# Moving the turn, the rank products, the scatters and the first block table of layer 0's routing to later places in a written-out order

## The chip, the cores and the metric

The kernel runs on one core of a Trainium2 chip. The metric is the device time of one execution in microseconds (us); lower is better. A core has five engines, each of which works through its own list of instructions in order: TensorE (PE, matrix products and transposes), VectorE (DVE), ScalarE (ACT), GpSimd (POOL) and SyncE (SP, which here only issues DMAs). The engines wait for each other through semaphores.

## The reference

Two layers, each of them a cross-attention and a mixture of experts, over 32 sequences of 128 tokens with 128 features; each sequence attends to a context of 77 rows. In float32:

```python
x = x + tanh(g_xattn[0]) * attn0(layernorm(x), ctx)    # 8 heads of 64
x = x + tanh(g_ffn[0])   * moe0(layernorm(x))          # 8 experts, top 2, silu(a) * b, biases
x = x + tanh(g_xattn[1]) * attn1(layernorm(x), ctx)    # 16 heads of 8
x = x + tanh(g_ffn[1])   * moe1(layernorm(x))          # 8 experts, top 2, gelu
```

In `moe0` the scores of a token are `x @ Wr.T + br`; the two experts with the largest `scores + biases_N` are taken, and their softmax weights are scaled to a sum of one.

## The kernel before, in words

All engines follow one list, `order()`. Each element is a task such as `("rank", 0, g)`; every engine loops over the whole list and issues its own part of each task, or nothing. The place of a task in the list is therefore its place in the queue of every engine that has a part in it. Semaphore waits inside the tasks keep the data right.

Layer 0's attention is made by `attention0_steps`, one step u for each sequence, and four more at the end that overlap with the experts. A step holds these tasks in this order:

- `score0(u)`: six matmuls (L977) into two PSUM banks, then VectorE's minimum of each row, `row_max` (L1475), and a subtraction (L1478)
- `k0`: products of the keys for the next group of four sequences (PE L914 to L916, a copy on ACT L1264, the remainder on VectorE L1444), in up to three places of a step, named by `more[0]` to `more[2]`
- `exp0(u)`: four exponentials on ACT (L1304) and one over the first half (L1308)
- `weigh0(u - 2)`: ten matmuls (L1019) and VectorE's addition to `x_res` (L1497)
- `v0`: one product of values (PE), copied out by ACT as `vo` (L1314) and stored by SP. A second one, in every fourth step, comes after `turn0`
- `divide0(u)`: VectorE's `row_sum` (L1488) and reciprocal (L1491), POOL's division of `prob` (L1846)
- `turn0(u - 1)`: ten transposes of the divided `prob` (L1001), copied out by ACT as `prob_t` (L1329)
- `bias0(u)`, the third `k0`, `norm` or `normalize` of the next group
- the routing tasks due in this step, `tasks.get(u, [])`

The routing tasks belong to layer 0's experts and run under the attention. For a group g of four sequences, whose attention is done by step 4g + 5, `route_tasks` puts them at steps u = 4g + 6 plus an offset from `steps0`:

- `mnorm` (0): VectorE's statistics, POOL's `m_rstd` (L1887, L1889)
- `mnormalize` (1): VectorE's `m_shift` (L1533), then ACT's four copies to `xm` (L1297)
- `mturn` (2): four transposes on PE (L1113), copied by ACT to `xm_t` (L1355)
- `route` (3): eight matmuls (L1121), then VectorE's `scores`, `ranked` and the eight largest
- `pick` (4): VectorE finds the two experts of each token and counts (L1564 to L1586), POOL L1896 and L1899
- `rank` (5): five matmuls (L1134 to L1137) that give each token its place with its expert, then four operations on VectorE (L1593 to L1601), the last of which writes `row`
- `lead` (6): the weights of the two experts
- `scatter` j = 0 to 3 (5, 6, 7, 8): two indirect DMAs each on POOL (L1918), which write the normalized rows to `x_rows` at the places in `row`; they wait for `row` and `xm`

After group 4 (FIRST_GROUPS) the first table of blocks is made: `totals` (5), one matmul and VectorE; `blocks` in three pieces (6, 6, 6), VectorE alone (L1679 to L1711); `block_bias` (7), PE matmuls (L1151) and a copy on VectorE (L1715). SP's `fetch` tasks, which begin at the end of step 31, need the table's `row_of` and the landed scatters of groups 0 to 4.

PSUM has eight banks, and `bank_of` names that of each task. `mturn`, `route` and `rank` of groups 0 to 4 and the first `totals` use V_BANK, the one of `v0`; for the later groups, and for `block_bias`, it is ROUTE_BANK. A task on PE waits until the previous user of its bank in the list has been read: for `rank` in its old place this is the `vo` copy of the same step. ACT's `vo` copy comes after `exp0` in ACT's queue, and `exp0` waits for `row_max`.

Of the kernel before, what the change touches and what calls it, by code (L numbers as in the profile page):

```python
# [35 lines left out]
GS = 4  # L36
# [84 lines left out]
def route_tasks(layer, spacing, lag, steps, tables):  # L121

    at = {}
    for g in range(NG):
        u = spacing * g + lag
        for kind, step in zip(("mnorm", "mnormalize", "mturn", "route", "pick", "rank", "lead"), steps[g][0]):
            if g >= ROUTED[layer] and kind == "rank":
                continue  # L130
            at.setdefault(u + step, []).append((kind, layer, g))
            if g >= ROUTED[layer] and kind == "lead":
                at.setdefault(u + step, []).append(("expert_w",))
        if g + 1 in PART_GROUPS[layer]:
            part = PART_GROUPS[layer].index(g + 1)
            total, table, bias = tables[part]
            at.setdefault(u + total, []).append(("totals", layer, part))
            for e in range(NEXP if part == PARTS - 1 else 0):
                at.setdefault(u + total + e // (2 + 2 * layer), []).append(("tail", layer, e))
            for piece, step in enumerate(table):  # L140
                at.setdefault(u + step, []).append(("blocks", layer, part, piece))
            if layer == 0:
                at.setdefault(u + bias, []).append(("block_bias", layer, part))
        for j, step in enumerate(steps[g][1] if g < ROUTED[layer] else ()):
            at.setdefault(u + step, []).append(("scatter", layer, g, j))

    last = ("blocks", "lead") if layer == 0 else ("scatter", "blocks", "expert_w")
    return {u: sorted(step, key=lambda t: t[0] in last) for u, step in at.items()}


def value_halves():

    begun, out = 2, []
    for u in range(NSEQ):
        last = ((min(u + 2, NSEQ) * NKEY) - 1) // P
        n = min(max(2 * (last + 1), (5 * (u + 1) + 13) // 4), 2 * CTX_BLOCKS)
        out.append([("v0", k // 2, k % 2) for k in range(begun, n)])
        begun = n  # L160
    return out


def attention0_steps(tasks):
    values = value_halves()
    background = [("ctx", i) for i in range(2, CTX_SETS)] + [("weights1",), ("tables", 0)]
    background += [("expert", 0, e) for e in range(NEXP)] + [("tables", 1)]
    for u in range(NSEQ + 4):
        step = []
        more = prepare_attention0_at(u) if u < NSEQ else ([], [], [], [])  # L170
        if u < NSEQ:
            step += [("score0", u)] + more[0] + [("exp0", u)]
        if 0 <= u - 2 < NSEQ:
            step.append(("weigh0", u - 2))
        if u < NSEQ:
            step += [("v0_load", u)] + values[u][:1] + [("divide0", u)] + more[1]
        if 0 <= u - 1 < NSEQ:
            step.append(("turn0", u - 1))
        if u < NSEQ:
            step += values[u][1:] + [("bias0", u)] + more[2]  # L180
        step += more[3] + tasks.get(u, [])
        if background:
            step.append(background.pop(0))
        if u == NSEQ - 1:
            step += [("fetch", i) for i in range(AHEAD)]
        yield step
# [41 lines left out]
def prepare_attention0(g):  # L228
    out = [("norm", g)]
    for head in range(NH0):  # L230
        out.append(("k0", g, head))
        if head == 2:
            out.append(("normalize", g))
        if head == 5:
            out.append(("xt", g))
    return out


def prepare_attention0_at(u):

    g = (u + 1) // GS + 1 if u >= GS - 1 else 1
    if g >= NG:
        return [], [], [], []
    keys = ((3, 2, 1, 2) if g > 1 else (3, 3, 2, 0))
    turn = u % GS
    before = sum(keys[i] for i in ((3, 0, 1, 2) if g > 1 else (0, 1, 2))[:(turn + 1) % GS if g > 1 else turn])
    places = [[("k0", g, before + n)] for n in range(keys[turn])]
    if turn == 2:
        places.append([("xt", g)])
    places += [[]] * (3 - len(places))  # L250
    return places + [[("norm", g)] if turn == 0 else [("normalize", g)] if turn == 1 else []]
# [29 lines left out]
def first_keys_and_queries():  # L281

    loads = [[[("k_load", g, piece)] for piece in range(6)] for g in (0, 1)]
    clears = [[("clear", 1, heads)] for heads in range(HEAD_SETS)] + [[], []]
    out = [[("v1_ones",)]] + [[("clear", 0, heads)] for heads in range(HEAD_SETS)] + [[("k1", 0)], []]
    for load, clear in zip(loads[0], clears):
        out += [load, clear]
    out += [[("k1", 1)], []]
    for load in loads[1]:
        out += [load, []]  # L290
    return out + [[("norm", NG)], [], [("normalize", NG)], [("xt", NG)], [("q1", 0)], [("q_load", 0)]]


def dense_tasks(experts):

    return [t for e in experts for t in (("dense_up", e, 0), ("dense_up", e, 1), ("dense_down", e))]
# [60 lines left out]
def order():  # L357

    first = prepare_attention0(0)
    out = [first[0], ("turn_weight", 0), ("turn_weight", 1), ("ctx", 0), ("wqk", 0), ("wqk", 1), ("turn_weight", 2)]  # L360
    out += first[1:] + [("wvo", 0), ("wvo", 1), ("ctx", 1), ("v0", 0, 0), ("v0", 0, 1), ("gates",)]
    steps0 = [((0, 1, 2, 3, 4, 5, 6), (5, 6, 7, 8))] * 5 + [((0, 1, 2, 3, 4, 5, 6), (5, 6, 7, 8)), ((0, 1, 2, 3, 3, 4, 5), (5, 5, 5, 5)), ((0, 1, 2, 3, 4, 5, 6), (5, 6, 7, 8))]
    steps1 = [((0, 1, 3, 5, 6, 7, 9), (9, 11, 13, 15))] * 5 + [((0, 1, 3, 5, 6, 7, 9), (8, 9, 10, 11)), ((0, 1, 2, 3, 4, 5, 6), (6, 6, 7, 7)), ((0, 1, 3, 5, 6, 7, 9), (9, 11, 13, 15))]
    tasks = [route_tasks(0, GS, 6, steps0, ((5, (6, 6, 6), 7), (5, (6, 6, 6), 7))),
             route_tasks(1, 2 * GS, 13, steps1, ((7, (8, 8, 8), 0), (5, (6, 6, 6), 0)))]
    after0 = [[("expert", 1, e)] for e in range(NEXP)] + first_keys_and_queries()
    phases = [(attention0_steps(tasks[0]), NSEQ), (expert_steps(0, tasks[0], NSEQ + 4, after0), BLOCKS[0] + 2),
              (attention1_steps(tasks[1]), U1 + 1), (expert_steps(1, tasks[1], U1 + 5, []), BLOCKS[1])]
    begun = 0
    for i, (phase, alone) in enumerate(phases):  # L370
        after = phases[i + 1][0] if i + 1 < len(phases) else iter(())
        for _ in range(alone - begun):
            out += next(phase)
        begun = 0
        for step in phase:
            out += step
            out += next(after, [])
            begun += 1
        if i + 1 < len(phases):
            out += next(after)  # L380
            begun += 1
    late = dense_tasks(range(DENSE_LATE, NEXP))
    out += late[:-1] + [("load_last", q) for q in range(LAST // 2)]
    out += late[-1:] + [("dense_out", j) for j in range(GS)] + [("combine_last", n) for n in range(LAST)]
    apart = {t[1:] for t in out if t[0] == "rest"}
    return [u for t in out for u in ([t, ("rest",) + t] if t[0] in SPLIT_KINDS and t not in apart else [t])]


def flamingo_two_layers(nc, a, out):
    plan = order()  # L390

    splits = [t for t in plan if t[0] in SPLIT_KINDS]
# [1562 lines left out]
```

## Time and profile before

| what | value |
|---|---|
| median of 3 runs | 788.54 us (787.5 to 790.2) |
| the profiled execution's own time | 795.85 us |
| its span, first to last instruction | 794.1 us |
| mean granted TensorE clock | 0.933 of full speed |
| PE busy | 647.0 us, 81% of the span |
| VectorE busy | 556.0 us, 70% |
| ScalarE busy | 442.0 us, 56% |
| GpSimd busy | 448.4 us, 56% |

The profiled execution is 7.3 us longer than the median, so differences are taken within it. Layer 0's attention fills the span up to about 240 us; the edit touches steps from 86 us on. Times in the rows below are microseconds from the start of the span.

### The profile page before, as it was taken

Reading aid. Unit: us, or ns where it says so; the run is one execution under the profiler, and the core shown is the slowest. Engines: PE = TensorE matmul, PEld = TensorE weight load, DVE = VectorE, ACT = ScalarE, POOL = GpSimd, SP = SyncE. Lnnn points to the kernel's source line nnn. Section 1 sums busy time; section 2 is a strip of 40 time slices with the busy share of each in tenths; the row PEclk is TensorE's granted clock in tenths of the full one; section 3 lists DMA queues with packets and bytes.
Section 4 is the critical chain, followed back from the end, with each engine's and each line's share of the span. In section 5 each row is a group of like instructions: output and inputs, shape, how many; then the busy total and the mean of one; then the engine's idle time right before and its main releaser. Section 6 shows DMA issues by size and latency. Waiting matters only on the chain.

```text
span 794.1 us, 16522 instructions
## 1 busy us (share of the span) xinstructions
PE 647.0 (81%) x4501; PEld 584.0 (74%) x4501; DVE 556.0 (70%) x1971; ACT 442.0 (56%) x1275; POOL 448.4 (56%) x665
## 2 busy tenths in 40 slices
PE   6888888899766767978688899889879875898886
PEld 5677778888666657877677788878768874787775
DVE  3367688887874566876787889888878755444564
ACT  2476767677434434655556776767665542433452
POOL 4035357776667565875445334767656665565541
PEclk9999999998978788999997999999999996999999
DMA  9446667454422223434352435535413013332444
GB/s 261 117 115 171 174 172 182 124 154 110 127 72 87 62 79 113 110 93 119 106 156 76 114 78 107 122 85 103 113 58 84 31 34 93 102 89 79 135 145 153
DMA packets 127383, 89.48 MB, mean 113 GB/s; under 512 B 30996, under 2 KB 116276, under 8 KB 127260
## 3 DMA queue, kind: packets, MB, share of 16 engines
q1 hardware_dynamic: 110844, 64.93, 32.1%
q0 software_dynamic: 8128, 17.65, 6.8%
q10 hardware_dynamic: 8320, 5.85, 2.6%
q8 instruction: 38, 0.62, 0.3%
q14 instruction: 53, 0.43, 0.2%
HBM read 50.73 MB, written 39.85 MB: 114 GB/s over the span
## 4 chain that ended last, share of the span: by engine, by line
PE 39%; DVE 21%; issue 12%; ACT 11%; SPq 5%; another core or an unknown queue 4%; DMA 3%; POOL 2%; DVEq 1%; ACTq 0%; POOLq 0%
PE banks L1171 7%; PE banks L1191 5%; PE banks L1034 5%; SPq L824 3%; DMA v_rows<-vo 3%; DVE row_max L1428 3%; PE banks L914 2%; PE banks L1001 2%; PE banks L977 2%; PE banks L1212 2%; PE banks L1019 2%; DVE hidden L1743 2%; DVE up L1735 2%; DVE x_res L1767 2%
## 5 line engine op out<-in xcount | busy, mean ns | idle before, releaser
L1925 POOL DMA_INDIRECT y_rows<-y_sb,result_at x134 | 131.1, 978 | 107.9 <-DVE result_at L1723 46.5
L1171 PE MATMUL banks<-xb,up 128*128 128x128 f32 x820 | 127.8, 297 | 47.1 <-DVE hidden L1743 22.4
L1171 PEld LDWEIGHTS banks<-xb,up 128*128 128x128 f32 x820 | 112.8, 207 | 61.5 <-issue 33.7
L1918 POOL DMA_INDIRECT x_rows<-xm,row x120 | 120.5, 1004 | 31.6 <-issue 28.5
L1880 POOL TENSOR_TENSOR v_flat<-v_raw,row_head 104x64 f32<-104x64 f32 (+1 forms) x128 | 55.6, 461 | 73.1 <-ACT v_raw L1345 72.1
L1191 PE MATMUL banks<-down,hidden 128*128 x536 | 87.6, 289 | 8.9 <-DVE y_sb L1760 4.6
L1329 ACT ACTIVATE prob_t<-banks 128x512 f32<-128x512 f32 x192 | 73.3, 439 | 28.7 <-PE banks L1001 24.8
L1034 PE MATMUL banks<-v_flat,prob_t 128*128 128x108 f32 (+2 forms) x640 | 86.5, 284 | 3.3 <-ACT prob_t L1329 1.3
L1034 PEld LDWEIGHTS banks<-v_flat,prob_t 128*128 128x128 f32 (+1 forms) x640 | 79.7, 197 | 10.6 <-ACT prob_t L1329 6.8
L1383 ACT ACTIVATE gate<-banks,block_bias 128x128 f32<-128x128 f32 x142 | 44.4, 365 | 76.2 <-PE banks L1171 44.7
L1191 PEld LDWEIGHTS banks<-down,hidden 128*128 128x128 f32 x536 | 75.0, 202 | 12.0 <-issue 12.0
L1846 POOL TENSOR_TENSOR prob<-prob,inv_sum 128x616 f32<-128x616 f32 x32 | 39.1, 1223 | 57.8 <-DVE inv_sum L1491 57.6
L1743 DVE SCALAR_TENSOR_TENSOR hidden<-banks,block_bias,gate 128x128 f32<-128x128 f32 x142 | 42.8, 343 | 33.8 <-ACT gate L1383 27.5
L1428 DVE TENSOR_REDUCE row_max<-banks 128x8 f32<-128x616 f32 x64 | 50.4, 788 | 9.3 <-PE banks L993 9.3
L1001 PE MATMUL banks<-ident,prob 128*128 128x128 f32 (+1 forms) x375 | 56.3, 283 | 0.0
L1019 PE MATMUL banks<-vo_flat,prob_t 128*128 128x128 f32 (+1 forms) x320 | 47.4, 302 | 8.6 <-ACT prob_t L1329 6.6
L1735 DVE COPY up<-up 128x256 f32 x134 | 49.5, 370 | 6.9 <-issue 2.4
L1019 PEld LDWEIGHTS banks<-vo_flat,prob_t 128*128 128x128 f32 (+1 forms) x320 | 45.2, 217 | 9.7 <-ACT prob_t L1329 7.4
L1387 ACT ACTIVATE hidden<-banks 128x256 f32<-128x256 f32 x63 | 24.0, 382 | 45.9 <-PE banks L1171 35.8
L1760 DVE COPY y_sb<-banks 128x128 f32<-128x128 f32 x63 | 18.1, 287 | 44.5 <-PE banks L1191 32.3
L1304 ACT ACTIVATE prob<-banks,row_max 128x77 f32<-128x77 f32 x128 | 30.8, 324 | 32.7 <-issue 20.4
L1001 PEld LDWEIGHTS banks<-ident,prob 128*128 128x128 f32 (+1 forms) x375 | 46.2, 147 | 0.8 <-issue 0.2
(238 smaller groups left out, 1657.9 us busy)
## 6 DMA issues: line engine op xcount, KB each, us to landing
vo_flat<-v_rows SPq DMA_DIRECT2D x32, 256.0 KB
x_norm<-x_rows SPq DMA_DIRECT2D x74, 72.0 KB
v_rows<-vo SPq DMA_DIRECT2D x38, 128.0 KB
x_far<-x_rows SPq DMA_DIRECT2D x60, 72.0 KB
gathered<-y_rows ACTq DMA_DIRECT2D x32, 128.0 KB
q_rows<-up_raw SPq DMA_DIRECT2D x8, 512.0 KB, 2.8
q_even<-q_rows SPq DMA_DIRECT2D x12, 256.0 KB
q_odd<-q_rows SPq DMA_DIRECT2D x12, 256.0 KB
```

Source lines behind the costliest of these rows:

```text
L1001: done = pe.transpose(banks[0:chunk_rows[c], PT_BANK[k], c % 4 * SEQ:(c % 4 + 1) * SEQ], flat[:, c * P:c * P + chunk_rows[c]], ident[:, :])
L1019: done = pe.matmul(banks[:, O_BANK, 0:D], prob_t[0:rows, b % 2, c, :], vo_flat[0:rows, b % 2, c, :], start=c == 0, stop=c == CHUNKS - 1)
L1034: done = pe.matmul(banks[:, O_BANK, half * width:half * width + cols], prob_t[0:rows, u % 2, c, :], v1_flat[0:rows, first:first + cols], s ...
L1171: done = pe.matmul(banks[:, UP_BANK[i % 2], part * P:(part + 1) * P], block_w[:, i % WR, part // 2, part % 2 * P:(part % 2 + 1) * P], xb[: ...
L1191: done = pe.matmul(banks[:, Y_BANK[i % 2], 0:D], hidden[:, i % HR, half, :], of_expert(flat[:, (2 * layer + half) * D:], i, D), start=half ...
L1329: act.activation(dst, banks[0:rows, PT_BANK[k], 0:len(chunks) * SEQ], ACT.Copy).then_inc(sem("prob_t"))
L1428: dve.tensor_reduce(m_view, s_view, AX.X, ALU.max).then_inc(sem("row_max"))
L1735: dve.tensor_copy(block_w[:, i % WR, 1 - layer, :], src[:, bass.ds(at, HID1)]).then_inc(sem("block_w_dve"))
L1743: dve.scalar_tensor_tensor(hidden[:, i % HR, half, :], banks[:, UP_BANK[i % 2], (2 + half) * P:(3 + half) * P], block_bias[:, k, 2 + half, ...
L1880: pool.tensor_tensor(v1_rows[0:rows, b % 2, half, chunks[0]:chunks[-1] + 1, :, 0:DK1], v1_raw[0:rows, chunks[0]:chunks[-1] + 1, half, :, : ...
L1918: pool.indirect_dma_start(out=x_rows[layer][:, :], out_offset=bass.IndirectOffsetOnAxis(ap=row[:, n, c:c + 1], axis=0), in_=xm[:, i % 2, j ...
L1925: pool.indirect_dma_start(out=y_rows[layer][:, :], out_offset=bass.IndirectOffsetOnAxis(ap=result_at[:, i % (2 * YR):i % (2 * YR) + 1], ax ...
```

## The change

```diff
@@ attention0_steps
         if 0 <= u - 1 < NSEQ:
             step.append(("turn0", u - 1))
+        step += tasks.get(u - 0.5, [])
         if u < NSEQ:
             step += values[u][1:] + [("bias0", u)] + more[2]
         step += more[3] + tasks.get(u, [])
@@ order
-    steps0 = [((0, 1, 2, 3, 4, 5, 6), (5, 6, 7, 8))] * 5 + [...]
+    steps0 = [((0, 1, 2.5, 3, 4, 5.5, 6), (6, 7, 7, 8))] * 5 + [...]
-    tasks = [route_tasks(0, GS, 6, steps0, ((5, (6, 6, 6), 7), (5, (6, 6, 6), 7))),
+    tasks = [route_tasks(0, GS, 6, steps0, ((6, (7, 8, 8), 9), (5, (6, 6, 6), 7))),
```

An offset with a half is served in the middle of the next step, right after `turn0`. For groups 0 to 4 `mturn` is now there in step 4g + 9 (`route` is still at the end of that step) and `rank` in step 4g + 12. The scatters j = 0 and 1 are one step later, j = 2 and 3 where they were. Of the first table, `totals` moves from step 27 to 28, the three pieces of `blocks` from 28 to 29, 30 and 30, `block_bias` from 29 to 31. Groups 5 to 7, the second table and layer 1 are untouched, and no instruction is added or dropped.

## Rows read from the trace of the kernel before

**Rows 1.** The page, part 4: the chain that ended last, by engine.

```profile
PE 39%; DVE 21%; issue 12%; ACT 11%; SPq 5%; another core or an unknown queue 4%; DMA 3%; POOL 2%; DVEq 1%; ACTq 0%; POOLq 0%
```

**Rows 2.** Waits, 60 to 290 us: total us, times, longest.

```profile
ACT prob L1304 <- issue: 20.4, 6, 4.1
...
PE banks L1134 <- ACT vo L1314: 13.3, 5, 3.2
```

**Rows 3.** Timeline, steps 19 and 20: start, length, what [idle before it <- releaser].

```profile
153.40 0.77 DVE L1475 TENSOR_REDUCE row_max<-banks 128x8 f32<-128x616 f32 x1
...
154.20 0.97 ACT L1304 ACTIVATE prob<-banks,row_max 128x77 f32<-128x77 f32 x4 [2.77 <-issue]
...
155.39 0.61 ACT L1314 ACTIVATE vo<-banks 128x512 f32<-128x512 f32 x1
...
156.14 0.25 PE L1134 MATMUL banks<-picked,earlier 128*128 128x32 f32 x1 [2.41 <-ACT vo L1314]
...
157.06 0.19 DVE L1593 TENSOR_TENSOR rank_row<-banks,region 128x32 f32<-128x32 f32 x1
...
158.34 0.16 DVE L1533 SCALAR_TENSOR_TENSOR m_shift<-m_mean_var,m_rstd 128x4 f32<-128x4 f32 x1
158.53 1.65 ACT L1297 ACTIVATE xm<-x_res,m_shift,m_rstd 128x128 f32<-128x128 f32 x4 [1.56 <-DVE m_shift L1533]
...
161.72 0.79 DVE L1488 TENSOR_REDUCE row_sum<-prob 128x8 f32<-128x616 f32 x1 [0.44 <-ACT prob L1308]
...
163.62 0.48 DVE L1444 TENSOR_TENSOR k_t<-banks,k_t 128x308 fp32r<-128x308 f32 x1 [0.52 <-ACT k_t L1264]
```

**Rows 4.** Windows, `row_max` of step 4k+3 to 4k+5: length, busy by engine, PEclk, DMA.

```profile
153.40:165.14 11.74, 9.33 (x61) 8.97 (x59) 9.47 (x31) 8.31 (x25) 7.62 (x11) 0.85 0.52 136
177.46:190.79 13.33, 10.93 (x61) 10.42 (x59) 9.44 (x31) 8.44 (x25) 7.63 (x11) 0.74 0.46 120
sum 49.43, PE 39.37 PEld 37.77 DVE 37.88 ACT 33.69 POOL 29.60; mean PE 9.84 PEld 9.44 DVE 9.47 ACT 8.42 POOL 7.40
```

**Rows 5.** Timeline, the turn and the route of group 3.

```profile
163.47 0.60 ACT L1355 ACTIVATE xm_t<-banks 128x512 f32<-128x512 f32 x1
...
167.16 0.61 ACT L1314 ACTIVATE vo<-banks 128x512 f32<-128x512 f32 x1
...
167.82 1.06 PE L1121 MATMUL banks<-router,xm_t 128*128 128x8 f32 x8 [0.33 <-ACT vo L1314]
...
167.94 0.80 ACT L1329 ACTIVATE prob_t<-banks 128x512 f32<-128x512 f32 x2
```

**Rows 6.** Windows, `row_max` to `row_max` over a route, groups 0 and 3.

```profile
91.95:97.22 5.27, 4.58 (x35) 4.22 (x34) 4.90 (x16) 3.51 (x11) 2.89 (x4) 1.00 0.67 180
165.14:169.87 4.73, 4.41 (x34) 4.02 (x33) 4.08 (x17) 4.37 (x14) 3.93 (x7) 1.00 0.55 152
```

**Rows 7.** Source line L1121, whole span: idle before it, us and times.

```profile
  ACT xm_t L1355: 2.0, 2
```

**Rows 8.** Windows of VectorE alone, step 27 to 31: length, busy, PEclk, DMA.

```profile
203.11:237.15 34.04, 25.76 (x94) 0.82 0.30 85
```

**Rows 9.** Timeline, the block bias and the route of group 5.

```profile
221.40 1.88 PE L1121 MATMUL banks<-router,xm_t 128*128 128x8 f32 x8 [2.77 <-DVE block_bias L1715]
...
223.32 0.19 DVE L1546 TENSOR_TENSOR scores<-banks,router_b 128x32 f32<-128x32 f32 x1 [1.97 <-PE banks L1121]
...
225.06 0.80 DVE L1475 TENSOR_REDUCE row_max<-banks 128x8 f32<-128x616 f32 x1 [0.92 <-PE banks L977]
...
227.19 0.35 DVE L1497 SCALAR_TENSOR_TENSOR x_res<-banks,gates,x_res 128x128 f32<-128x128 f32 x1 [0.82 <-PE banks L1019]
```

**Rows 10.** Source line L1918, 100 to 235 us: ns min/median/max.

```profile
L1918 POOL DMA_INDIRECT x_rows<-xm,row x40: 957/995/1236, 109.7 to 231.7; - x40
```

**Rows 11.** Timeline of POOL, steps 21 and 22.

```profile
172.89 0.96 POOL L1918 DMA_INDIRECT x_rows<-xm,row  x1 [0.30 <-issue]
...
178.97 1.05 POOL L1889 TENSOR_TENSOR m_rstd<-m_rstd,minus_half 128x4 f32<-128x4 f32 x1
```

More of the change, by code:

```diff
@@ L361, in order @@
     out += first[1:] + [("wvo", 0), ("wvo", 1), ("ctx", 1), ("v0", 0, 0), ("v0", 0, 1), ("gates",)]
-    steps0 = [((0, 1, 2, 3, 4, 5, 6), (5, 6, 7, 8))] * 5 + [((0, 1, 2, 3, 4, 5, 6), (5, 6, 7, 8)), ((0, 1, 2, 3, 3, 4, 5), (5, 5, 5, 5)), ((0, 1, 2, 3, 4, 5, 6), (5, 6, 7, 8))]
+    steps0 = [((0, 1, 2.5, 3, 4, 5.5, 6), (6, 7, 7, 8))] * 5 + [((0, 1, 2, 3, 4, 5, 6), (5, 6, 7, 8)), ((0, 1, 2, 3, 3, 4, 5), (5, 5, 5, 5)), ((0, 1, 2, 3, 4, 5, 6), (5, 6, 7, 8))]
     steps1 = [((0, 1, 3, 5, 6, 7, 9), (9, 11, 13, 15))] * 5 + [((0, 1, 3, 5, 6, 7, 9), (8, 9, 10, 11)), ((0, 1, 2, 3, 4, 5, 6), (6, 6, 7, 7)), ((0, 1, 3, 5, 6, 7, 9), (9, 11, 13, 15))]
-    tasks = [route_tasks(0, GS, 6, steps0, ((5, (6, 6, 6), 7), (5, (6, 6, 6), 7))),
+    tasks = [route_tasks(0, GS, 6, steps0, ((6, (7, 8, 8), 9), (5, (6, 6, 6), 7))),
              route_tasks(1, 2 * GS, 13, steps1, ((7, (8, 8, 8), 0), (5, (6, 6, 6), 0)))]
```

## The prediction

> **What bounds the kernel now.** I read the page first, then the waits, then the stretch that the edit touches, engine by engine. The chain that ended last [rows 1] is spread over TensorE (PE), VectorE (DVE), "issue" and ScalarE (ACT): no engine is the bound by itself, so a saved microsecond counts only where a wait ends on it. The list of waits of layer 0's attention [rows 2] names the candidate: the rank products (L1134) stood 13.3 us, five times, for the copy of `vo` (L1314), which frees the one PSUM bank they share. Just above stand 20.4 us in which ACT had not begun `exp0` (L1304). The second explains the first, and the reader is to see it in [rows 3], step 19, the rank step of group 2. VectorE comes to the step's minimum (`row_max`, L1475) only at 153.40, because it still works on the picks and statistics of the step before. So ACT begins `exp0` at 154.20, copies `vo` at 155.39, and PE, idle for 2.41 us, starts the ranks at 156.14. VectorE then makes rows of them from 157.06 until `m_shift` at 158.34, ACT waits 1.56 us for `m_shift`, normalizes `xm`, and only then gets to the exponentials of step 20: `row_sum` at 161.72. The wait on PE is thus a result of VectorE's lateness, and the chain goes through VectorE and ACT. What I price is therefore the interval from one `row_max` to a later one. Step s is the s-th of the attention's steps, k0 the products of keys.
>
> **What the edit moves.** Nothing is added to or taken from the work. For groups 0 to 4 the turn of `xm` (four transposes on PE, one copy `xm_t` on ACT) goes from the end of step 4g+8 to the middle of 4g+9, where the route stays at the end; the ranks (five matmuls, four VectorE operations) go from the end of step 4g+11 to the middle of 4g+12; of the four scatter tasks (two indirect DMAs each, on POOL) the first two go one step later, so that step 4g+13 has two. The first table (totals, three pieces, block bias) goes from steps 27, 28, 29 to 28, 29, 30, 31.
>
> **The ranks, four times (groups 0 to 3).** Without the rank rows `m_shift` can come right after the k0 remainder at about 156.95, 1.4 us earlier (158.34 less 156.95; the four rank operations with their waits took 157.06 to 158.34 = 1.28 us). ACT's `xm`, `exp0` and `vo` and VectorE's `row_sum` all come 1.4 us earlier [rows 3]. Then the 1.28 us of rank rows come back, before the last k0 remainder of step 20, which stood idle for 0.52 us before it began at 163.62 [rows 3]. It takes up that gap: 1.4 - 1.28 + 0.52 = 0.64 us gained, of a stall of 2.41. PE now waits for the `vo` of step 20 instead: done with the turn at about 159.8, bank free at about 160.8, so about 1 us idle in place of 2.41. The four stretches from step 4k+3 to 4k+5 last 11.74 us for the one just worked through, 13.33 for the last, 49.43 in all [rows 4]: 49.43 - 4 x 11.74 = 2.47 us more than four of the middle one. In the last, PE's granted clock is 0.74 of full speed against 0.85, that is, it spent more time at the 1.2 GHz level after its idle stretch. With a stall of 1 us I expect it to stay at 2.4 GHz, and the excess to go. Together 4 x 0.64 + 2.47 = 5.0 us gained. Bounds: below, 1.0 (VectorE full, only part of the excess comes back); above, 13.3 (the whole wait [rows 2]).
>
> **The turn, five times.** This is the price. Today `xm_t` is copied at 163.47 in 0.60 us, where ACT has time, and the route at 167.82 waits only for `vo` (0.33 us) [rows 5]. Now the turn itself waits for the `vo` copy that ends at 167.77, and ACT has a k0 copy and two `prob_t` copies, until 168.74, before it comes to `xm_t`. The route directly behind on PE waits for that: 168.74 + 0.60 = 169.34 in place of 167.82, 1.5 us. After the route come three VectorE operations and then `row_max` of the next step, with nothing to hide behind; the stretch today takes 4.73 us [rows 6]. That such a wait exists is seen elsewhere in this trace: two routes waited for `xm_t`, 2.0 us together [rows 7]. In the first group the stretch is already 5.27 us [rows 6] since VectorE has a slow operation there; 0.5 us of the 1.5 is hidden by it. Sum: 4 x 1.5 + 1.0 = 7.0 us lost. Bounds: 0 (if the step found other cover) and 8.
>
> **The table and the last rank step.** From `row_max` of step 27 (203.11) to the rows of group 5 (237.15) VectorE is busy for 25.76 of 34.04 us [rows 8]. Its work is only dealt out differently, so what counts is the idle time. The block bias in front of the route of group 5 shares a bank with it: PE stood idle 2.77 us and came back at the low level of its clock (the eight matmuls took 1.88 us), VectorE stood idle 1.97, 0.92 and 0.82 us, 3.7 in all [rows 9]. With the block bias two steps later the route runs at once: 3.7 us gained. The new place of the block bias is in front of group 5's ranks, in step 31, same bank: its copy on VectorE, then five matmuls at the low clock, and VectorE waits about 1.1 us. Net 2.6 us gained; bounds 0.5 and 4.5. Groups 5 to 7 stay where they are, fetches wait for rows of the table at step 30 instead of 28, and begin in step 31 as before: nothing, unless the table ends late, which the gain here excludes.
>
> **The scatters.** POOL has the division of every step as well, and PE turns that result. Two more indirect DMAs now stand in front of the division of step 22. One takes 0.995 us [rows 10] and the queue 0.30 us to the next [rows 11], so POOL comes 2.6 us later to that division and to `m_rstd`, the last of what `m_shift` waits for. It ended at 180.02 (178.97 + 1.05 [rows 11]); with POOL's start 0.6 us earlier, 182.0. VectorE would ask for it 3.55 us after its `row_max`, at 177.46 + 0.86 + 3.55 = 181.9 (0.86 being 1.5 lost less 0.64 gained). So the cover is used up: 0.1 us late, four times, 0.4 us. The division itself has about a microsecond left.
>
> The Trainium skill bears on this. The 40 scatters of this attention took 957 to 1236 ns, whatever VectorE did beside them [rows 10]. "SBUF — State Buffer", section "SBUF: two separate sides", says that an indirect DMA issued from POOL can't write its descriptors while VectorE runs a copy that takes both ports, and gives 620 ns alone against about 3100 beside such a copy. By that rule the two added scatters could cost up to 5 us each time; the trace disagrees, and the sum goes by the rows.
>
> **Sum.** 7.0 + 0.4 - 5.0 - 2.6 = -0.2 us. It is made against the profiled execution, which took 795.85 us with a span of 794.1, 7.3 us above the median of the runs, 788.54; all terms are differences of short stretches, so I carry -0.2 over as it is: 788.3 us.
>
> **Rivals.** (a) *The turn is hidden*: ACT reaches `xm_t` sooner, or PE has other work. Then 7.0 falls away: 781.3 us. For it: PE waits only 0.33 us at the route now. Against: nothing stands between turn and route in the new order. 0.14. (b) *The rank wait comes back in full*: 13.3 in place of 5.0: 780.0 us. For it: it is the longest wait of PE. Against: [rows 3], VectorE and ACT are the late ones. 0.10. (c) *POOL becomes the bound*, the case on the other side. `m_rstd` passes 3.55 us after `row_max`; from there each microsecond costs four. If the six scatters ahead of it take 1.236 instead of 0.995 us, it is 1.4 us later, 5.8 us in all: 794.1 us. For it: the cover is gone. Against: the median lies near the low end of its rows. The skill's rule above would make this case larger. 0.12. (d) *The rank rows eat all that they free*: VectorE is full in step 20, and only the lower bound of 1.0 comes back: 792.3 us. For it: VectorE's idle time there is only 0.52 us. Against: the excess of the fourth stretch is PE's. 0.14. Left for the forecast: 0.50, with a range of its own of 785.5 to 791.
>
> **Numbers.** A measurement here can't tell less than 0.3%, 2.4 us: 786.1 to 790.9. Of the forecast's 0.50 I put 0.40 within, 0.08 below, 0.02 above; (a) and (b) give 0.24 faster, (c) and (d) 0.26, of which 0.03 within. Faster 0.32, same 0.43, slower 0.25. The range takes in (a), (d) and most of the bounds of the terms, 781 to 793: beyond it lie (b) and the far half of (c).
>
> **What the changed profile would show.** No PE wait of 2.4 us before L1134 but one of about 1 us, still on `vo`; in front of L1121 a new wait of about 1 us on `xm_t`, five times; stretches of 11.1 us (4k+3 to 4k+5) and 6.2 us (4k+5 to 4k+6); no wait of L1121 on `block_bias`, but one of L1134. I am wrong if L1121 doesn't wait for `xm_t`, if the stretches with the ranks shrink by over 2 us each, or if ACT's wait for `m_shift` ends on POOL.

## The result, and the profile after

The changed kernel took 800.3 us (median of 4 runs, 796.34 to 804.69) against 789.37 for the kernel before (4 runs, 787.5 to 793.14): a ratio of 1.0127 [1.0085, 1.0169], so 1.3% slower, clear of 1. The forecast was 788.3 with a range of 781 to 793. Here and below, a run more than 1.5% above the fastest of its kernel is left out of the ratio, though not of the median. The profiled execution took 804.69 us, its span 803.0 (before 795.85 and 794.1). Line numbers after L176 are those of before plus one. The chain that ended last, against [rows 1], has more of PE and of VectorE and nothing new in it:

```profile
PE 41%; DVE 25%; ACT 13%; issue 11%; another core or an unknown queue 3%; POOL 2%; SPq 1%; DMA 1%; DVEq 1%; ACTq 0%; POOLq 0%
```

The waits of layer 0's attention, 60 to 300 us, against [rows 2] (total, times, longest):

```profile
ACT prob L1305 <- DVE row_max L1476: 17.4, 10, 8.1
...
DVE scores L1547 <- PE banks L1122: 8.3, 6, 1.6
...
ACT xm L1298 <- DVE m_shift L1534: 7.5, 6, 3.0
...
PE banks L1114 <- ACT vo L1315: 5.4, 5, 1.2
...
PE banks L1135 <- ACT vo L1315: 3.2, 3, 1.6
```

PE's wait in front of the ranks did go, from 13.3 to 3.2 us. But the same list has a wait that the list of before has not, of the next score matmuls for VectorE's subtraction:

```profile
PE banks L978 <- DVE prob L1479: 10.6, 6, 3.0
```

So most of PE's idle time moved and did not go away.

The windows from `row_max` of step 4k+3 to that of 4k+5, middle and last stretch and the sum of all four, against [rows 4]:

```profile
162.36:174.38 12.02, 9.77 (x59) 8.94 (x60) 10.29 (x32) 7.82 (x24) 5.54 (x9) 0.86 0.41 108
189.21:201.67 12.46, 10.50 (x56) 9.81 (x57) 9.95 (x31) 8.04 (x24) 5.54 (x9) 0.73 0.40 104
sum 48.50, PE 39.35 PEld 36.16 DVE 40.79 ACT 31.50 POOL 21.15; mean PE 9.84 PEld 9.04 DVE 10.20 ACT 7.87 POOL 5.29
```

The sum is 48.50 us, not 49.43: 0.93 gained where 5.0 were forecast. The middle stretch is even longer than before, 12.02 against 11.74, and PE is idle in it for 2.25 us (12.02 less 9.77) where before it was idle for 2.41 (11.74 less 9.33). VectorE has the same work but is busy for 10.29 us instead of 9.47, and the timeline of GpSimd, VectorE, ACT and PE in the stretch shows on what:

```profile
163.70 0.55 PE L978 MATMUL banks<-k_t,xt_h 128*128 128x308 f32 x2 [2.06 <-DVE prob L1479]
...
165.63 1.21 POOL L1847 TENSOR_TENSOR prob<-prob,inv_sum 128x616 f32<-128x616 f32 x1 [0.71 <-DVE inv_sum L1492]
...
165.81 1.05 DVE L1534 SCALAR_TENSOR_TENSOR m_shift<-m_mean_var,m_rstd 128x4 f32<-128x4 f32 x1
166.78 0.79 DVE L1476 TENSOR_REDUCE row_max<-banks 128x8 f32<-128x616 f32 x1
...
166.90 1.65 ACT L1298 ACTIVATE xm<-x_res,m_shift,m_rstd 128x128 f32<-128x128 f32 x4 [0.96 <-DVE m_shift L1534]
...
170.68 0.25 PE L1135 MATMUL banks<-picked,earlier 128*128 128x32 f32 x1 [0.66 <-ACT vo L1315]
```

`m_shift`, 128x4 elements, took 0.16 us before [rows 3] and takes 1.05 now, in each of the groups 1 to 4. It starts 0.18 us after GpSimd's division and ends at 166.86, when the division does (166.84). ACT's `xm` waits for it. The rank rows are now beside the next step's division (171.19 to 172.41), and one of them, `rank_hot` with two inputs in SBUF, took 0.86 us there (0.85, 0.85, 0.86 and 0.37 in the four stretches, before 0.39, 0.41, 0.68 and 0.54; 0.23 with nothing of GpSimd's beside it).

**The turn.** The route of group 3, with its window, against [rows 5, 6]:

```profile
177.16 0.63 PE L1114 MATMUL banks<-ident,xm 128*128 128x128 f32 x4 [1.19 <-ACT vo L1315]
178.52 1.06 PE L1122 MATMUL banks<-router,xm_t 128*128 128x8 f32 x8 [0.74 <-issue]
...
179.62 0.19 DVE L1547 TENSOR_TENSOR scores<-banks,router_b 128x32 f32<-128x32 f32 x1 [1.61 <-PE banks L1122]
...
174.38:180.57 6.19, 4.26 (x31) 3.71 (x30) 4.21 (x16) 5.31 (x16) 5.41 (x8) 1.00 0.46 120
```

PE waits 1.19 us in front of the turn and 0.74 between turn and route, where the trace names no releaser for this group but `xm_t` for group 0 below, and the copy of `xm_t` ended just before (at 178.47); VectorE waits 1.61 us for the scores. The stretch takes 6.19 us instead of 4.73; the four of groups 1 to 4 are 1.61, 1.46, 1.46 and 1.45 us longer. Group 0, forecast at 1.0 us, loses more: `row_max` of step 9 to 10 is 2.51 us longer (7.78 against 5.27) and 10 to 11 another 1.36, and its route runs at the low level of PE's clock, eight matmuls in 1.88 us where group 3's took 1.06. The granted clock of these two stretches is 0.77 and 0.81, before 1.00 in both:

```profile
96.34 1.88 PE L1122 MATMUL banks<-router,xm_t 128*128 128x8 f32 x8 [0.73 <-ACT xm_t L1356]
```

**The picks.** From 4k+2 to 4k+3 the forecast had nothing, and the stretch is 1.04, 1.05, 1.05 and 1.06 us longer (8.64 against 7.59). GpSimd and VectorE in step 22:

```profile
184.64 0.96 POOL L1919 DMA_INDIRECT x_rows<-xm,row  x1 [0.30 <-issue]
185.63 1.22 POOL L1847 TENSOR_TENSOR prob<-prob,inv_sum 128x616 f32<-128x616 f32 x1
...
185.20 1.69 DVE L1567 CAST top_idf<-top_idx 128x8 f32<-128x8 uint32 x1
```

The operands of that division had been ready since 183.78 (the end of `inv_sum`). Four indirect DMAs, from 180.77 to 185.60, stood in front of it, two more than before. VectorE's cast of the picks, 0.64 us before, takes 1.69 and ends at 186.89, with the division (186.85).

**The table.** VectorE from `row_max` of step 27 to the rows of group 5, against [rows 8], and PE's and VectorE's waits in it, against [rows 9]:

```profile
216.50:250.21 33.71, 25.06 (x94) 0.74 0.31 90
...
238.27 1.86 DVE L1567 CAST top_idf<-top_idx 128x8 f32<-128x8 uint32 x1
...
244.13 1.91 PE L1152 MATMUL banks<-bias_pick,up_raw 8*128 8x33 f32 x8 [3.22 <-DVE bias_pick L1704]
248.07 0.37 PE L1135 MATMUL banks<-picked,earlier 128*128 128x32 f32 x1 [2.02 <-DVE block_bias L1716]
```

The block bias has left the route and stands in front of the ranks, as forecast. But 33.71 us are only 0.33 less than 34.04.

The sum of it, by differences of the two timelines at `row_max`: 0.27 before step 9, 2.51 + 1.36 in group 0, 5.98 in the four turn stretches, 4.20 in the four of the picks, -0.93 in the four of the ranks, -0.33 in the last part. That is 13.06 us late when group 5's rows are written (250.21 against 237.15; the stretches of the turn, the picks and the ranks are those of groups 1 to 4). About 4 us come back during layer 0's experts, which I did not follow further; the span is 8.9 us longer.

### The profile page after: what moved, and what is told of

Read it like the earlier page. It is cut to its first block, busy times and chain, and to the rows that moved or that the text cites. A ratio compares the mean times of both kernels' runs of the same rounds, so it can differ in the third digit from the quotient of the medians.

```text
span 803.0 us, 16522 instructions
## 1 busy us (share of the span) xinstructions
PE 656.9 (82%) x4501; PEld 589.6 (73%) x4501; DVE 564.5 (70%) x1971; ACT 444.0 (55%) x1275; POOL 447.4 (56%) x665
## 4 chain that ended last, share of the span: by engine, by line
PE 41%; DVE 25%; ACT 13%; issue 11%; another core or an unknown queue 3%; POOL 2%; SPq 1%; DMA 1%; DVEq 1%; ACTq 0%; POOLq 0%
PE banks L1172 8%; PE banks L1192 5%; PE banks L1035 5%; DVE row_max L1429 3%; PE banks L915 2%; PE banks L1020 2%; PE banks L917 2%; PE banks L1213 2%; ACT prob L1305 2%; PE banks L1002 2%; PE banks L978 2%; DVE x_res L1768 2%; PE banks L1122 2%; PE banks L916 2%
## 5 line engine op out<-in xcount | busy, mean ns | idle before, releaser
L1172 PE MATMUL banks<-xb,up 128*128 128x128 f32 x820 | 129.5, 299 | 43.5 <-DVE hidden L1744 17.0
L1736 DVE COPY up<-up 128x256 f32 x134 | 51.3, 383 | 7.0 <-issue 2.6
```

The lines of the kernel that those rows point to most:

```text
L1172: done = pe.matmul(banks[:, UP_BANK[i % 2], part * P:(part + 1) * P], block_w[:, i % WR, part // 2, part % 2 * P:(part % 2 + 1) * P], xb[: ...
L1736: dve.tensor_copy(block_w[:, i % WR, 1 - layer, :], src[:, bass.ds(at, HID1)]).then_inc(sem("block_w_dve"))
```

## The experiments

Each kernel was timed against the kernel before on its own chip. That took 744.83, 793.1, 792.49 and 791.12 us in the four sets of runs, so ratios are compared, and stretches of the traces. "16 steps" is `row_max` of step 11 to that of step 27, four whole groups, and "ranks" the four stretches from 4k+3 to 4k+5 in it.

| kernel | set | ratio | ranks, us | 16 steps, us | cast, groups 1 to 4 | `m_shift`, groups 1 to 4 |
|---|---|---|---|---|---|---|
| before | | 1 | 49.43 | 98.72 | 0.65, 0.64, 0.64, 0.62 | 0.15, 0.16, 0.16, 0.16 |
| changed | | 1.0127 | 48.50 | 107.97 | 1.84, 1.49, 1.69, 1.70 | 1.05 x4 |
| turn alone | 1 | 1.0077 | 47.02 | 103.04 | 0.36, 0.17, 0.34, 0.17 | 0.15, 0.16, 0.16, 0.16 |
| ranks and scatters alone | 1 | 1.0081 | 54.42 | 105.79 | 0.17, 1.20, 0.17, 0.17 | 0.68, 1.18, 1.05, 1.18 |
| table alone | 1 | 0.9976 | 48.99 | 98.28 | 0.63, 0.64, 0.65, 0.62 | 0.15, 0.16, 0.16, 0.16 |
| table alone, again | 3 | 0.9955 | 48.01 | 97.32 | 0.64, 0.65, 0.65, 0.64 | 0.15, 0.16, 0.16, 0.16 |

**One part at a time.** The turn alone:

```diff
-    steps0 = [((0, 1, 2, 3, 4, 5, 6), (5, 6, 7, 8))] * 5
+    steps0 = [((0, 1, 2.5, 3, 4, 5, 6), (5, 6, 7, 8))] * 5
```

> The kernel before with only the turn of groups 0 to 4 half a step later. Theory L (part of the loss is the turn's wait, the rest is VectorE standing behind GpSimd's division in its small operations): the route waits about 0.7 us for xm_t behind a turn that waits about 1.2 us for vo; row_max of step 4k+1 to 4k+2 takes 6.2 us for 4.73, and 7.8 for 5.27 in the first group; the other stretches stay as before, and the cast of pick stays at 0.65 us or less. Total 6 to 8 us over the kernel before. Theory W (waits alone, all of the loss is the turn): the same stretches, but about 11 us in total. Theory P (the turn is hidden): 0.

Ratio 1.0077 [1.0048, 1.0106], 5.7 us of 744.83. Two of its stretches 4k+1 to 4k+2, at the high level of the clock, look as in the changed kernel:

```profile
118.15:124.35 6.20, 4.59 (x34) 4.01 (x33) 4.21 (x16) 5.31 (x16) 5.41 (x8) 1.00 0.64 165
...
169.68:175.89 6.21, 4.62 (x34) 4.02 (x33) 4.22 (x16) 5.31 (x16) 5.41 (x8) 1.00 0.45 119
```

So the price of the turn is its own. The total is a little under the 6 to 8 us expected. The other stretches did not stay as before: the four of the ranks, whose place is the old one here, are 11.76, 11.75, 11.77 and 11.74 us, 47.02 in all. The excess of 2.47 us of [rows 4] can go without moving the ranks.

The ranks and scatters alone:

```diff
-    steps0 = [((0, 1, 2, 3, 4, 5, 6), (5, 6, 7, 8))] * 5
+    steps0 = [((0, 1, 2, 3, 4, 5.5, 6), (6, 7, 7, 8))] * 5
```

> The kernel before with only the ranks half a step later and the scatters in their new places. Theory L: m_shift of VectorE now starts beside the division and takes 1.05 us for 0.16, so that the stretch from row_max of step 4k+3 to 4k+5 is about 12.0 us (sum of four 48.5 for 49.4); the cast of pick meets the division of step 4k+2 and takes 1.5 us or more for 0.65, so that row_max of 4k+2 to 4k+3 takes 8.6 for 7.6. Total 2 to 6 us over the kernel before. Theory W: stretches of 11.1 us, no change of 4k+2 to 4k+3, and 4 to 5 us under the kernel before.

Ratio 1.0081 [1.0054, 1.0108]: the half that was forecast to gain 4.6 us costs 0.81%. The expectation had the sign but only part of the account: the ranks' stretches add up to 54.42 us and not 48.5, and only one of the four casts is slow. In two of the four stretches `m_shift` comes late, as rival (c) had it; GpSimd's `m_rstd`, behind the scatters, ends only when VectorE has long asked:

```profile
132.16 1.05 POOL L1890 TENSOR_TENSOR m_rstd<-m_rstd,minus_half 128x4 f32<-128x4 f32 x1
133.19 1.21 POOL L1847 TENSOR_TENSOR prob<-prob,inv_sum 128x616 f32<-128x616 f32 x1
...
133.24 1.18 DVE L1534 SCALAR_TENSOR_TENSOR m_shift<-m_mean_var,m_rstd 128x4 f32<-128x4 f32 x1 [1.95 <-POOL m_rstd L1890]
```

It then pays twice, 1.95 us of waiting and 1.18 beside the division. The table alone, twice:

```diff
-    route_tasks(0, GS, 6, steps0, ((5, (6, 6, 6), 7), (5, (6, 6, 6), 7)))
+    route_tasks(0, GS, 6, steps0, ((6, (7, 8, 8), 9), (5, (6, 6, 6), 7)))
```

> The kernel before with only the first table later. Forecast on record: 2.6 us faster. After the result: the route of group 5 no longer waits for block_bias, the ranks of group 5 do, about 2 us; row_max of step 27 to the rows of group 5 takes 33 to 34 us for 34.04; total between 1.5 us faster and 1 us slower.

> Kernel before with the first table's steps alone moved, on another chip and with more rounds: the ratio was 0.9976 [0.9948, 1.0004]. If the block bias away from the route of group 5 gains what the trace showed (row_max of step 27 to the rows of group 5 in 32.5 us, not 34.0), the ratio is 0.998 with an interval below 1; if it is nothing, 1.000.

Ratios 0.9976 [0.9948, 1.0004] and 0.9955 [0.9929, 0.9982]. The first interval takes in 1, and in the second set the plain medians, 791.45 and 792.49, make 0.9987. So a small gain is likely, and its size is not settled. The first trace has 32.50 us and the second 31.93 us of VectorE's stretch where before had 34.04 (the window below ends 0.08 us before the rows are written), the second with PE's matmuls of the block bias at the high level of the clock:

```profile
201.65:233.50 31.85, 25.46 (x93) 0.82 0.35 99
...
227.50 1.07 PE L1151 MATMUL banks<-bias_pick,up_raw 8*128 8x33 f32 x8 [2.36 <-DVE bias_pick L1703]
231.44 0.37 PE L1134 MATMUL banks<-picked,earlier 128*128 128x32 f32 x1 [2.86 <-DVE block_bias L1715]
```

This part of the change, by itself, is the only version with a ratio below 1. The three parts add up, 0.77 + 0.81 - 0.35 = 1.23% against 1.27 measured, but that is in part luck: most of what the second part loses by itself is the late `m_rstd`, which the changed kernel has not, and the changed kernel loses instead at the picks.

**Is it the division that holds VectorE up?** The cast was made by another operation, in the changed kernel:

```diff
-dve.tensor_copy(top_idf[:, s, :, :], top_idx[:, s, :, 0:2])
+dve.tensor_reduce(top_idf[:, s, :, :], top_idx[:, s, :, 0:2].unsqueeze(3), AX.X, ALU.max)
```

> The changed kernel with the cast of the two expert numbers made by a reduction over one element, on the same operands. Theory L (VectorE's copies and its operations with two inputs in SBUF stand until GpSimd's division is over, a reduction doesn't): the reduction takes 0.2 us beside the division, and the next operation, the copy of token_at into xm, takes the wait: about 1.5 us for 0.38. row_max of 4k+2 to 4k+3 stays at 8.6 us. Rival C (the cast itself is slow, or the reading of uint32): the copy stays at 0.38 us and the stretch falls to about 7.2 us.

One run: 803.87 us, with 793.1 for the kernel before on that chip. The picks of step 22, VectorE and then GpSimd:

```profile
184.45 0.16 DVE L1567 TENSOR_REDUCE top_idf<-top_idx 128x8 f32<-128x8 uint32 x1
184.65 1.25 DVE L1571 COPY xm<-token_at 128x4 f32<-128x4 f32 x1
...
184.64 1.22 POOL L1847 TENSOR_TENSOR prob<-prob,inv_sum 128x616 f32<-128x616 f32 x1
```

The reduction takes 0.16 us in every group; the copy behind it, 0.38 us in the changed kernel, takes 1.25, the length of the division at its side. So it isn't the conversion that is slow, but whichever copy comes beside the division. This reduction was over before the division began. That a reduction passes is seen in step 14: it began 0.38 us into the last indirect DMA, the division right behind, and took 0.16 us, where the changed kernel's cast at 0.40 us took 1.84; the copy after it took 1.67. The other VectorE operations agree. In the sixteen traces `row_sum`, a reduction of `prob` in SBUF, took 0.78 to 0.80 us beside a division (3 cases) and 0.80 without, and `k_t<-banks,k_t`, with one input in PSUM, at most 0.48 beside one (88 cases) and without, while `rank_hot`, with both inputs in SBUF, took 0.23 alone and up to 1.29. The four stretches of the picks fell only from 34.6 us to 33.1 (8.51, 8.51, 8.28, 7.78), about as expected.

**The scatters' places.** Two orders of the changed kernel's scatter tasks:

```diff
-(6, 7, 7, 8)
+(6, 6, 7, 8)      first
+(6, 7, 8, 8)      second
```

> The changed kernel with scatter 1 in the step of scatter 0 (offsets 6, 6, 7, 8 for 6, 7, 7, 8), so that only two indirect DMAs stand between the divisions of steps 4k+1 and 4k+2. Theory L: GpSimd comes to the division of step 4k+2 before VectorE comes to the cast, the cast takes 0.65 us or less for 1.5 to 1.9, row_max of 4k+2 to 4k+3 falls from 8.65 to 7.6, four or five times: 4 to 5 us under the changed kernel. Rival R (the cast is slow for what VectorE or the route's delay does, not for where GpSimd is): the cast stays at 1.5 to 1.9 and the time at that of the changed kernel.

> The changed kernel with scatter 2 one step later as well (offsets 6, 7, 8, 8). The run with offsets 6, 6, 7, 8 left six indirect DMAs in front of the division of step 4k+2, as in the changed kernel; here there are four, as in the kernel before. Theory L: the division of step 4k+2 starts when inv_sum is there, about 2 us earlier, and is over or nearly so when VectorE comes to the cast: the cast takes 0.2 to 0.65 us for 1.5 to 1.9, row_max of 4k+2 to 4k+3 takes 7.2 to 7.7 us for 8.64. m_rstd still has six in front of it, so the turn's 1.5 us in each period must still cover it. Total 3 to 5 us under the changed kernel. Rival R (the cast's length has nothing to do with the division): it stays at 1.5 to 1.9 us and the time at that of the changed kernel.

The first changed nothing beyond the noise, ratio 1.0181 [1.0127, 1.0234], casts 1.84, 1.70, 1.69, 1.69: just as many indirect DMAs, six, stand in front of the division of step 4k+2 as before the edit. The expectation had not counted them. The second, 1.0200 [1.0148, 1.0251], removed one pair from there and did what it was meant to at that place: casts 0.17, 0.17, 0.34, 0.32 and stretches of 7.90, 8.84, 7.13 and 7.13 us, 31.0 in place of 34.6. The 8.84 is not VectorE's: PE is busy for all of it, at a granted clock of 0.78. But two tasks in 4g+14 make `m_rstd` late, and the rank stretches grow from 48.5 to 52.2 us:

```profile
193.73 1.18 DVE L1534 SCALAR_TENSOR_TENSOR m_shift<-m_mean_var,m_rstd 128x4 f32<-128x4 f32 x1 [1.32 <-POOL m_rstd L1890]
```

Four tasks at one a step, up to 4g+15, in the kernel before with the ranks moved, and in the changed kernel:

```diff
-(6, 7, 7, 8)
+(6, 7, 8, 9)
```

> Kernel before with the ranks of groups 0 to 4 half a step later, as in the change, and all four scatter tasks one step later (4g+12 to 4g+15), so that every step keeps one task. Turn and table stay. Theory L (small VectorE operations lose time beside a GpSimd operation on tensors; scatters hurt only where two tasks fall in one step): the cast takes 0.17 to 0.65 us, not 1.2 and above; m_shift takes about 1.05 us since it still starts beside the division; the four stretches 4k+3 to 4k+5 make about 48 us together (before 49.4); 4k+2 to 4k+3 stays at 7.6; ratio 0.996 to 1.000. Rival S (the ranks half a step later cost by themselves, whatever the scatters): four stretches 52 or more, ratio 1.004 and above.

> Changed kernel with the four scatter tasks at one a step (4g+12 to 4g+15). Theory L: the cast takes 0.17 to 0.65 us, and 4k+2 to 4k+3 goes back from 8.64 to about 7.6 us, without the late m_rstd that two tasks in the last step gave; m_shift stays near 1.05 and 4k+1 to 4k+2 at 6.2 us. Some 4 to 5 us less than the changed kernel: ratio about 1.006 to 1.008. Rival (the turn's new place makes 4k+2 to 4k+3 longer by itself): it stays at 8.6, ratio 1.012 and above.

Both are far slower, 1.0309 [1.0269, 1.0350] and 1.0355 [1.0316, 1.0394], and no theory had it. In the first, ACT stands still before the normalization:

```profile
138.18 1.65 ACT L1298 ACTIVATE xm<-x_res,m_shift,m_rstd 128x128 f32<-128x128 f32 x4 [6.20 <-DMA x_rows<-xm,row]
```

`xm` has two buffers. The normalization of group g+2, in step 4g+15, writes the one that the scatter of group g still reads. So the ranks at 4g+12 leave three steps for four scatter tasks, and one step must take two. The small operations were short (casts of 0.17 to 0.77 us), but nothing follows for the ranks' own price, since the new wait covers it.

**`m_shift` made by GpSimd.** Right behind `m_rstd`, in the changed kernel, in the kernel before, in the kernel before with ranks, spaced scatters and table, and in the changed kernel with the turn put back (scatters as in the change, and at 6, 6, 7, 8):

```diff
-dve.scalar_tensor_tensor(m_shift[:, i % 2, :], m_mean_var[:, :, 0], -1.0, m_rstd[:, i % 2, :], ALU.mult, ALU.mult)
+pool.tensor_scalar(m_shift[:, i % 2, :], m_mean_var[:, :, 0], -1.0, None, ALU.mult)
...
+pool.tensor_tensor(m_shift[:, i % 2, :], m_shift[:, i % 2, :], r, ALU.mult)
```

> The changed kernel with m_shift made by GpSimd behind m_rstd (two small operations more on GpSimd, one fewer on VectorE, which had two inputs in SBUF and started beside the division). Theory L: row_max of step 4k+3 to 4k+4 falls from 4.42 to 3.5 us, ACT normalizes xm about 1 us earlier, and the stretch 4k+3 to 4k+5 falls from 12.0 to about 11.1 us, the 11.1 of the forecast. Total 3 to 4 us under the changed kernel. Rival V (VectorE is full there anyway): stretch 12.0, no change.

> The kernel before with m_shift made by GpSimd behind m_rstd, nothing else. There m_shift takes 0.16 us but stands behind the rank rows on VectorE, so ACT normalizes xm only at 158.53 where m_rstd is ready at 155.96. Theory M (ACT's wait for m_shift is on the chain): xm at about 156.7, exp0 of step 4k+4 right after row_max, 0.7 us earlier, four or five times: 2 to 4 us under the kernel before. Rival V (VectorE's own work sets it): no change within 1 us.

> As the run before it in this list, and m_shift made by GpSimd behind m_rstd, and the first table's steps as in the change. Theory L: no VectorE operation is left that is queued behind the division in the rank's stretch, so the four stretches make 43.8 us together (10.95 each); 4k+1 to 4k+2 stays at 4.7 us because PE has no idle stretch at the turn; 27 to 31 about 27 us; ratio 0.990 to 0.994, which would beat both kernels. Rival K (what is gained in the rank's stretch is given back in another one, as it was with the turn moved): ratio 0.998 to 1.003, with one of the other stretches longer by about 1 us in each group.

> Kernel before with the ranks, scatters (4g+12, 4g+13 twice, 4g+14) and table of the change, and m_shift made by GpSimd; the turn stays at the end of 4g+8. If the turn's idle time on PE is what gave the gain back in the changed kernel with m_shift on GpSimd: 4k+1 to 4k+2 is 4.7 to 5.0 us instead of 7.7, the four stretches 4k+3 to 4k+5 make 43.8 us, 4k+2 to 4k+3 stays at 8.6 us where the scatters push the division into the picks: in all 5.6 less and 4.2 more and 2 less from the table, ratio 0.993 to 0.998. Rival (the late m_rstd seen with the turn at its old place decides): m_shift on GpSimd comes late, two of the four stretches are 14 us or more, ratio 1.002 to 1.010.

> The same with the scatters at 4g+12 twice, 4g+13, 4g+14. If GpSimd's room behind the division of 4k+2 decides whether m_rstd is late, this one is in time (one task in 4g+13): four stretches 43.8 us, none above 12, ratio 0.990 to 0.997. Rival (six indirect DMAs ahead of that division in either order): no difference between the two runs.

| kernel, `m_shift` on GpSimd | set | ratio | ranks, us | 16 steps, us |
|---|---|---|---|---|
| changed | 2 | 1.0194 [1.0132, 1.0255] | 43.79 | 107.74 |
| before | 2 | 1.0031 [0.9998, 1.0063] | 49.23 | 98.62 |
| ranks, spaced scatters, table | 3 | 1.0336 [1.0285, 1.0387] | 64.39 | 117.42 |
| changed, turn put back | 4 | 1.0066 [1.0028, 1.0104] | 50.02 | 102.93 |
| the same, scatters 6, 6, 7, 8 | 4 | 1.0074 [1.0034, 1.0113] | 46.93 | 103.68 |

In the changed kernel the four stretches of the ranks become 10.94, 10.94, 10.95 and 10.96 us: what the forecast had said (11.1) and 4.7 less than the changed kernel's. This shows what `m_shift` beside the division costs. In the kernel before, where `m_shift` took 0.16 us, the same edit gained nothing, against an expectation of 2 to 4 us: ACT's wait for `m_shift` fell from 12.2 to 1.5 us and the ranks' stretches stayed at 49.23 us. That wait was not what set their length. The changed kernel with the edit gained nothing as a whole either, for the stretches 4k+1 to 4k+2 of groups 2 to 4 grew to 7.73, 7.69 and 7.62 us. The windows 4k to 4k+1 and 4k+1 to 4k+2 of this kernel, and those of the changed kernel:

```profile
162.14:169.65 7.51, 6.74 (x50) 6.36 (x51) 6.17 (x23) 5.06 (x16) 3.08 (x4) 1.00 0.52 143
169.65:177.34 7.69, 5.76 (x30) 5.21 (x29) 4.08 (x16) 5.30 (x16) 6.48 (x9) 0.78 0.42 107
```

```profile
166.78:174.38 7.60, 6.94 (x49) 6.53 (x48) 6.17 (x23) 5.04 (x15) 2.10 (x4) 0.92 0.40 102
174.38:180.57 6.19, 4.26 (x31) 3.71 (x30) 4.21 (x16) 5.31 (x16) 5.41 (x8) 1.00 0.46 120
```

PE's granted clock is 0.78 in the turn's stretch, with the same two idle times around the turn (1.19 and 0.74 us), and its eight route matmuls take 1.77 us instead of 1.06. In the changed kernel the low level had come in the stretch before. The low level then lasts through the picks of this kernel. Three of its four casts are short again (0.17 us), yet the stretches of the picks stay at 34.56 us, for another reason: PE is busy for all of the last three, at a granted clock of 0.80 to 0.81 where the changed kernel had 1.00.

```profile
177.34:185.94 8.60, 8.60 (x51) 8.08 (x51) 6.33 (x31) 4.34 (x12) 6.70 (x8) 0.80 0.40 113
```

So here each microsecond freed on VectorE was lost again on PE. What makes the low level come in one stretch and not in another, with the same idle times, no run told apart.

In the kernel with spaced scatters ACT again stood for `xm`'s buffer, 29.1 us in five waits, and it tells nothing more. For the changed kernel's loss I then took the turn's idle time for the one cause, and was wrong. With the turn put back neither kernel beats the kernel before. In the first, two of the four rank stretches are 13.94 and 13.78 us, with GpSimd late:

```profile
133.79 1.65 ACT L1298 ACTIVATE xm<-x_res,m_shift,m_rstd 128x128 f32<-128x128 f32 x4 [2.21 <-POOL m_shift L1892]
```

In the second none is above 12.02, but the sixteen steps are 4.96 us longer than before all the same: ranks -2.50, picks +2.82 (33.19 against 30.37), turn stretches +4.64 (23.56 against 18.92). In one of these last, 7.42 us long, PE is never idle:

```profile
141.14:148.56 7.42, 7.42 (x55) 7.10 (x55) 4.34 (x15) 5.03 (x15) 6.06 (x9) 0.95 0.49 137
```

It has 55 PE records where [rows 6] has 34: work that the stretch before, 132.58 to 141.14, at a granted clock of 0.84, had not got through. What the ranks at half a step later cost by themselves, with GpSimd in time and no collision, stays open: no order with two buffers of `xm` gave such a kernel, and a third buffer was not tried.

## Why the prediction was wrong

**What bounds the kernel, and the first wait: right in part.** PE's wait in front of the ranks fell to about a microsecond, as forecast (0.66 us in the group shown, 3.2 in all). That PE was waiting for a late VectorE is borne out too, for it now waits for VectorE at the score matmuls, 10.6 us in all. The forecast did not see that wait. It expected PE to keep the high level of its clock with only 1 us idle; PE stood 2.06 us in front of L978, and the granted clocks of the four stretches are 1.00, 0.86, 0.86 and 0.73, before 0.86, 0.86, 0.85 and 0.74. The excess, forecast to go for that reason, shrank from 2.47 to 0.42 us (48.50 less 4 x 12.02) all the same, most of it in the last stretch, whose clock did not rise. It also went with the turn alone. That part of the gain came out by luck.

**The turn: right.** 1.5 us a group forecast, 1.45 to 1.61 measured, by the waits named, on `vo` and then on `xm_t`. Alone it costs 0.77%, which is 6.1 us of 789.37, forecast 7.0. In the changed kernel the first group was taken too low, 1.0 against 3.9 us, as its route and what follows fell to the low level of the clock.

**The table: about right alone.** 2.6 us forecast; 0.24 and 0.45%, 1.9 and 3.6 us, by the ratios, and 1.54 and 2.11 us in the stretches of the two traces. In the changed kernel, 0.33 us: against the second of these traces the cast is 1.08 us longer there (1.86 against 0.78), and the block bias's matmuls 0.84 (1.91 against 1.07).

**The ranks: the step that failed.** "Without the rank rows `m_shift` can come right after the k0 remainder" is what happened. That it would then take the 0.16 us of [rows 3] did not. The division waits for `inv_sum`, two VectorE operations ahead of that place, so that GpSimd always begins it there. Before, the rank rows (1.28 us) lay between and let the division pass; they were not only in the way. Of the 4.07 us missing (5.0 less 0.93), 4 x 0.89 = 3.6 is `m_shift`: the stretch forecast at 11.10 us took 12.02, and 10.95 once `m_shift` was off VectorE. The 0.64 us to be gained in the middle stretch came out as 0.28 lost (12.02 less 11.74). The rows for it stood in the trace of before. The slow operation to which the forecast put the first group's 5.27 us is `shift_n`, of the same kind and size as `m_shift`, and it stood beside a division; the later ones of its kind took 0.15 us:

```profile
95.22 1.22 POOL L1846 TENSOR_TENSOR prob<-prob,inv_sum 128x616 f32<-128x616 f32 x1 [1.75 <-DVE inv_sum L1491]
95.39 1.05 DVE L1470 SCALAR_TENSOR_TENSOR shift_n<-mean_var,rstd 128x4 f32<-128x4 f32 x1
```

Part of the 1.28 us of rank rows was that too: `rank_hot` at 157.28 took 0.68 us beside the division (156.66 to 157.88), 0.23 alone. And the timeline has the cast of step 22, 0.64 us where group 0's took 0.17, ending at 175.14, with the division's 175.10:

```profile
173.86 1.24 POOL L1846 TENSOR_TENSOR prob<-prob,inv_sum 128x616 f32<-128x616 f32 x1
...
174.50 0.64 DVE L1566 CAST top_idf<-top_idx 128x8 f32<-128x8 uint32 x1
```

The Trainium skill, "SBUF — State Buffer", section "Who interferes with whom", states it: a VectorE instruction with two inputs in SBUF contends with a GpSimd instruction that reads SBUF, copies and casts can too, `tensor_reduce` does not, and the later one is blocked for the whole instruction. The traces agree on which operations are held and which are not: `m_shift` 0.16 to 1.05 us, cast up to 1.86, reduction 0.16. The casts that began before the division are taken up in the last section. The prediction had used the page only for the other direction, GpSimd held up by VectorE; the scatters took 954, 964 and 1237 ns (least, median, most), as in [rows 10].

**The scatters: mis-sized, and looked for at the wrong place.** The forecast counted 0.4 us at `m_rstd`, and let the division be late at no cost. This is the second step that failed, a term put at nothing. In the changed kernel `m_rstd` is in time (it ends at 191.77, `m_shift` starts at 192.65), and the late division meets the picks' cast: 4.20 us, four times the 1.05 by which the cast is longer (1.69 less 0.64). Rival (c), with `m_rstd` late, appears only once the turn is at its old place or step 4g+14 has two tasks.

**The rivals.** (a) and (b) fell. (d) had the gain of the ranks right, 1.0 against 0.93, but put it down to a full VectorE; VectorE was busy for 0.73 us more in each stretch (40.79 less 37.88, by four), no more than `m_shift`'s 0.89. (c) had the sign and, for another wait, about half of the loss: 794.1 is 5.6 us above the median of before, and 10.9 were measured. With the measured terms in place of the forecast's, alone, 6.1 + 6.4 - 2.8 = +9.7 us, against 10.9 between the medians; the middle term has another cause in the changed kernel, as said above.

## What to carry to other kernels

An operation between two others may be the cover that keeps a third from meeting a neighbour engine. Before moving it, look at what GpSimd runs in the place where the next VectorE operation will land, and price small VectorE operations there at the length of that GpSimd operation. When transfers are pushed later, count both ends: what is queued behind them on their engine, and which buffer's next writer they run into. And a large named wait (13.3 us here) is no gain: removing three quarters of it was worth 0.93 us, as 10.6 us came back in front of another instruction of the same engine. Compare an engine's idle time over the whole stretch, not one row of the waits.

## What was not expected of the hardware

VectorE operations of 4 to 8 elements a partition took as long as was left of GpSimd's 128x616 `tensor_tensor` beside them: 0.16 to 1.05 or 1.18 us (`scalar_tensor_tensor`), 0.17 to 1.20 (cast), 0.17 to 1.25 (copy), while a reduction kept its length.

A cast or copy can be held by an indirect DMA as well. From the ranks and scatters alone, with no division near:

```profile
178.31 0.96 POOL L1919 DMA_INDIRECT x_rows<-xm,row  x1 [0.30 <-issue]
...
178.67 0.17 DVE L1567 CAST top_idf<-top_idx 128x8 f32<-128x8 uint32 x1
178.87 0.36 DVE L1571 COPY xm<-token_at 128x4 f32<-128x4 f32 x1
```

The cast began 0.36 us into the DMA and took 0.17; the copy began 0.56 into it and took 0.36, to 0.04 us before the DMA's end (179.27). In the sixteen traces the copies that began 0.54 to 0.71 us into an indirect DMA, with no division behind it, took 0.28 to 0.39 us, until just before its end; one `scalar_tensor_tensor` at 0.60 us took 0.16. In the changed kernel the cast of step 22 began 0.56 us into the last DMA and the division followed at once, so the DMA's end and then the division held it, 1.69 us in all. Casts and copies that began only 0.35 to 0.42 us into a DMA took 0.16 to 0.18 us where no division followed, and 1.82 to 1.90 where one did (nine cases). Why the division to come mattered to them, no run told apart.
